# Feed-forward rows halved in row layout and turned by DMA instead of on TensorE

## The chip, the cores and the metric

The kernel runs on one NeuronCore of a Trainium2 chip. The metric is the device time of one execution in microseconds (us). The engines are TensorE (PE, with its weight loads shown as PEld), VectorE (DVE), ScalarE (ACT), GpSimd (POOL) and SyncE (SP), which here only issues DMAs.

## The reference

A gated block of a vision-language model, on 8 sequences of 224 rows of 2048 values, everything in float32:

```
x = x + tanh(g_xattn) * cross_attention(layernorm(x), ctx, ctx)     # 32 heads of 64, 8 shared key/value groups, 750 context rows
x = x + tanh(g_ffn) * ffn(layernorm(x))

ffn(h):  query = h @ Wq.T                       # 2048 -> 64
         top 8 of 512 router scores of query; softmax over those 8 slots gives w
         aux = (w @ aux_values) @ Wvd.T @ Wvu.T
         u = uncertainty(h)                     # variance of h, and gelu(h @ Wu1.T + bu1) @ Wu2.T, 2048 -> 512 -> 1
         return h + gate(u) * aux
```

Where bf16 is fed to TensorE, a float32 value is halved into a bf16 high part and a bf16 rest (value minus high part), and the product is summed from high*high, high*rest and rest*high.

## The kernel before

The attention takes the first 900 us or so and the change does not touch it. The feed-forward part then works on 14 tiles of 128 rows. Each engine has its own instruction stream written out by hand; the streams meet in semaphores, and an engine runs its stream strictly in order. After a lead-in for tiles 0 and 1 the streams have a loop `for t in range(1, TILES)`; loop t is called "loop t" below. It holds, for tile t, the query projection (`sum_query`), the wide projection (`sum_wide`), the router and the selection of 8 slots (`route`, `select`, `weigh`), for tile t - 1 the rest of the chain (`preact`, `gelu`, `dot`, `turn_w`, `sum_z`), and for tile t + 1 the preparation of the normed rows h. Loops 1 to 5 also carry the layer-norm statistics of later tiles on DVE (`late_stats`, two tiles a loop). Loops 8 to 13 and the part behind the loops carry the results of two tiles each (`FINISH`): eight quarters of 512 columns, each three matmuls on PE (`aux_part`), then one DVE instruction that adds it to the rows (`finish`); ACT prepares each of these tiles with one pass over its 2048 columns (`base`), and SP stores each finished tile.

The preparation of h is done in four quarters of 512 columns, j = 0 to 3. Before the change a quarter goes through these steps:

- `stage_h` (L1254, DVE): h = (x - mean) * rstd as float32, row layout, into `h_rows`, two buffers.
- `turn_h` (L953, PE): four float32 transposes of 128 by 128 into PSUM bank j % 2.
- `round_h` (L679, ACT): PSUM to bf16, the high part `h_hi`. It waits for the transposes and for `w1_quarter`, since tile t's `sum_wide(t, j)` must have read the quarter that is overwritten. There is one buffer per quarter.
- `split_h` (L1273, DVE): PSUM minus high part, to bf16 `h_lo`.
- `sum_query` (L980) and `sum_wide` (L966) on PE multiply the two parts.

`preact(t)` (L1362, DVE) empties the bank of `sum_wide(t, ...)` and `sum_wide(t + 1, 0)` waits for it; so in loop t the first quarter of `sum_wide` waits for `preact(t - 1)`, which is the first DVE instruction of the loop. `join_query` is L1366, `select` L1342 to L1354, `split_z` L1387, statistics L1240 and L1246, `finish` L1383 and `aux_part` L1044. On ACT, `gelu` is L766, `weigh` L770, `base` L745, `round_z` L778. All results' quarters but the last ones share PSUM bank 7, so that a quarter's matmuls wait for the DVE pass over the quarter before.

SP waits for each finished tile of `ORDER` and stores 1 MB (L490). The last two tiles are stored in quarters.

Of the kernel before, what the change touches and what calls it, by code (L numbers as in the profile page):

```python
# [5 lines left out]
ALU = mybir.AluOpType  # L6
# [62 lines left out]
def flamingo_block(nc, x_top, x_rest, k_t, v_rows, mask, g_x, av_t, wvd_t, w1_t, wq_t, wr, wr_rows_in, keys_t, log_rel, rel, b1, w2, wvu_t,  # L69
                   scalars, spill, out):  # L70
    with ExitStack() as ctx:
# [107 lines left out]
        h_rows = carve("ffn", [128, 2, 512])  # L179
        h_hi = carve("ffn", [128, 4, 4, 128], BF16)  # L180
        h_lo = carve("ffn", [128, 4, 4, 128], BF16)
        stage_at = used["ffn"] + 3 * HID
# [116 lines left out]
        h_hi_done = sem("h_hi_done")  # L299
        h_split = sem("h_split")  # L300
        w1_quarter = sem("w1_quarter")
        query_quarter = sem("query_quarter")
# [77 lines left out]
        def parts_before(u, n):  # L380
            return 4 * ORDER.index(u) + n

        TAIL_BANKS = {(TILES - 2, 0): 7, (TILES - 2, 1): 0, (TILES - 2, 2): 1, (TILES - 2, 3): 3,
                      (TILES - 1, 0): 4, (TILES - 1, 1): 5, (TILES - 1, 2): 2, (TILES - 1, 3): 7}

        def aux_ps(u, n):
            return psum[:, TAIL_BANKS.get((u, n), 7), :]

# [4 lines left out]
        def _(sp):  # L393
# [104 lines left out]
        def _(pool):  # L498
# [108 lines left out]
            pool.tensor_tensor(keys_lo[:, :], keys_raw, keys_hi[:, :], ALU.subtract).then_inc(keys_split, 1)  # L607

            for t in range(EARLY, TILES):
                root2(t, t + 1)  # L610

            pool.wait_ge(rstd2_done, TILES)
# [45 lines left out]
        def _(act):  # L658
# [16 lines left out]
            def round_h(t, j):  # L675
                act.wait_ge(h_turned, 4 * t + j + 1)
                if t >= 1:
                    act.wait_ge(w1_quarter, 4 * (t - 1) + j + 1)
                act.activation(h_hi[:, j], psum[:, j % 2, :].rearrange("p (k n) -> p k n", k=4), ACT.Copy).then_inc(h_hi_done, 1)  # L679

# [112 lines left out]
            for t in range(1, TILES):  # L793
                if t + 1 <= TILES:
                    round_h(t, 3)
                if t == 1:
# [5 lines left out]
                if t + 1 < TILES:  # L802
                    round_h(t + 1, 0)
                if t == LOG_STEP:
# [32 lines left out]
        def _(pe):  # L837
# [108 lines left out]
            def turn_h(t, j):  # L946
# [7 lines left out]
                mm.then_inc(h_turned, 1)  # L954

            def sum_wide(t, j, halves=range(2)):
                if 0 in halves:
                    pe.wait_ge(h_split, 4 * t + j + 1)
                    if t == 0:
                        pe.wait_ge(w1_split, 4 * j + 4)  # L960
                    if j == 0 and t >= 1:
                        pe.wait_ge(preact_done, t)
                for kk in range(2 * halves[0], 2 * halves[-1] + 2):
                    k = 4 * j + kk
                    for n, (h, w) in enumerate(((h_hi, high(w1_raw[:, k, :])), (h_hi, w1_lo[:, k, :]), (h_lo, high(w1_raw[:, k, :])))):
                        mm = pe.matmul(psum[:, 2, :], h[:, j, kk, :], w, start=(k == 0 and n == 0), stop=(k == KC - 1 and n == 2))  # L966
                if 1 in halves:
                    mm.then_inc(w1_quarter, 1)

            def sum_query(t, j):  # L970
                pe.wait_ge(h_split, 4 * t + j + 1)
                if t == 0 and j == 0:
# [47 lines left out]
            def aux_part(t, i):  # L1020
# [7 lines left out]
                if n == 0:  # L1028
                    pe.wait_ge(z_split, u + 1)
                bank = TAIL_BANKS.get((u, n), 7)  # L1030
                if bank == 7 and parts_before(u, n) >= 1:
                    last = parts_before(TILES - 2, 1) if (u, n) == (TILES - 1, 3) else parts_before(u, n)
                    pe.wait_ge(y_added, last)
                elif bank in (0, 1):
                    pe.wait_ge(h_split, 4 * TILES)
                elif bank == 3:
# [64 lines left out]
            for t in range(1, TILES):  # L1101
                last = t == TILES - 1
                sum_query(t, 0)
# [11 lines left out]
                sum_wide(t, 1, range(1, 2))  # L1115
                if not last:
                    turn_h(t + 1, 1)
                aux_part(t, 3)
# [4 lines left out]
                sum_wide(t, 2, range(1, 2))  # L1123
                if not last:
                    turn_h(t + 1, 2)
                aux_part(t, 5)
# [5 lines left out]
                sum_wide(t, 3, range(1, 2))  # L1132
                if not last:
                    turn_h(t + 1, 3)
                aux_part(t, 7)
# [10 lines left out]
        def _(dve):  # L1146
# [100 lines left out]

            def stage_h(t, j):
                rows = rows_of(t)
                if j == 0:  # L1250
                    dve.wait_ge(rstd2_done, t + 1)
                if t >= 1 or j >= 2:
                    dve.wait_ge(h_turned, 4 * t + j - 1)
                dve.tensor_scalar(h_rows[:, j % 2, :], rows[:, 512 * j:512 * j + 512], mv_all[:, t, 0:1], rstd_all[:, t:t + 1],  # L1254
                                  ALU.subtract, ALU.mult).then_inc(h_staged, 1)

            def next_stats(window, m):
# [153 lines left out]
            split_h(1, 2)  # L1411
            stage_h(2, 0)
            join_query(0)
            split_query(0)

            for t in range(1, TILES):
                preact(t - 1)
                finish(t - 1, 7)
                late_stats(t - 1, 7)
                split_h(t, 3)  # L1420
                if t + 1 < TILES:
                    stage_h(t + 1, 1)
                finish(t, 0)
# [4 lines left out]
                if t + 1 < TILES:  # L1428
                    split_h(t + 1, 0)
                    stage_h(t + 1, 2)  # L1430
                finish(t, 1)
# [8 lines left out]
                if t + 1 < TILES:  # L1440
                    split_h(t + 1, 1)
                    stage_h(t + 1, 3)
                finish(t, 3)
# [5 lines left out]
                if t + 1 < TILES:  # L1449
                    split_h(t + 1, 2)  # L1450
                if t + 2 < TILES:
                    stage_h(t + 2, 0)
                finish(t, 5)
# [91 lines left out]
```

## Time and profile before

| what | us |
|---|---|
| median of 3 runs (lowest, highest) | 1191.7 (1190.68, 1191.79) |
| the profiled execution's own time | 1189.83 |
| its span, first to last instruction | 1187.9 |
| busy in the span: PE, DVE, ACT, POOL | 1141.3, 946.4, 918.8, 888.4 |
| mean granted TensorE clock | 0.999 of full speed |

The span is what the profiler saw between the first and the last instruction; the execution's own time is 1.93 us longer. Busy time is the time in which an engine had an instruction under way; PE's is modelled from pipelined matmuls, so the distance between starts says more than the duration.

### The profile page before, as it was taken

The page shows a single profiled execution, that of the slowest core. Times are in us where ns is not written, and L with a number is a line of the kernel's source. Part 1 is how long each engine was busy: PE and PEld are TensorE (multiplying, and loading weights), DVE is VectorE, ACT ScalarE, POOL GpSimd, SP SyncE. Part 2 cuts the span into 40 slices and gives each one's busy share as a digit, 9 for nine tenths or more (in the row PEclk, how much of TensorE's full clock was granted, in tenths as well). Part 3 has the DMA queues.
Part 4 walks back from the last instruction along what each step waited for, and adds up shares of the span by engine and source line. Part 5 has one row for each costly group of instructions (what it writes and reads, how often), then busy time and mean ns, then how long its engine had stood idle before and what let it go on. Part 6 is the DMA issues. An engine that isn't in the chain of part 4 may idle for free.

```text
span 1187.9 us, 35060 instructions
## 1 busy us (share of the span) xinstructions
PE 1141.3 (96%) x14385; PEld 912.3 (77%) x14642; DVE 946.4 (80%) x2255; ACT 918.8 (77%) x1230; POOL 888.4 (75%) x797
## 2 busy tenths in 40 slices
PE   4999999999999999999999999999999999999997
PEld 3888888888888888888888888888877565555553
DVE  5988888887888888888888888888874888766765
ACT  5898998988988898898898889989862344555544
POOL 5999999999999999999999999999970001503222
PEclk9999999999999999999999999999999999999999
DMA  9421231142124213311421221131237100011223
GB/s 340 141 68 48 62 110 54 42 107 71 41 55 103 75 41 68 116 48 41 104 71 52 58 58 42 50 73 47 70 103 262 81 1 1 1 72 72 107 107 142
DMA packets 60735, 95.09 MB, mean 80 GB/s; under 512 B 35233, under 2 KB 44449, under 8 KB 56482
## 3 DMA queue, kind: packets, MB, share of 16 engines
q1 hardware_dynamic: 59858, 91.79, 25.1%
q8 instruction: 118, 1.93, 0.7%
q10 hardware_dynamic: 720, 1.05, 0.3%
q14 instruction: 39, 0.32, 0.1%
HBM read 71.75 MB, written 20.97 MB: 78 GB/s over the span
## 4 chain that ended last, share of the span: by engine, by line
PE 70%; POOL 16%; DVE 8%; issue 3%; ACT 2%; DMA 1%; DVEq 0%; SPq 0%; POOLq 0%
PE psum L913 13%; PE psum L890 12%; POOL arena L577 11%; PE psum L966 8%; PE psum L920 6%; PE psum L901 6%; PE psum L943 6%; PE psum L937 5%; PE psum L938 5%; PE psum L1044 2%; POOL arena L545 2%; PE psum L868 2%; PE psum L953 1%; PE psum L980 1%; POOL arena L594 1%
## 5 line engine op out<-in xcount | busy, mean ns | idle before, releaser
L577 POOL TENSOR_TENSOR arena<-arena 128x768 bf16<-128x768 f32 x448 | 652.6, 1472 | 43.4 <-ACT arena L699 41.5
L1283 DVE CUSTOM_DVE_ANT_0 arena<-psum,arena 128x750 f32<-128x750 f32 x448 | 420.5, 939 | 127.7 <-PE psum L901 122.0
L699 ACT ACTIVATE arena<-psum 128x768 f32<-128x768 f32 x448 | 362.6, 809 | 87.8 <-PE psum L920 87.7
L703 ACT ACTIVATE arena<-arena,neg_max 128x750 f32<-128x750 f32 x448 | 410.9, 917 | 4.2 <-DVE neg_max L1283 4.2
L913 PE MATMUL psum<-ident,arena 128*128 128x128 f32 x1792 | 268.4, 272 | 0.0
L937 PEld LDWEIGHTS psum<-arena 128*128 128x128 bf16 (+1 forms) x2688 | 194.7, 98 | 57.5
L890 PE MATMUL psum<-arena 128*128 128x512 bf16 x674 | 221.9, 383 | 14.2
L938 PE MATMUL psum<-arena 128*128 128x64 bf16 (+1 forms) x2688 | 222.0, 193 | 0.0
L937 PE MATMUL psum<-arena 128*128 128x65 bf16 (+1 forms) x2688 | 221.7, 194 | 0.0
L938 PEld LDWEIGHTS psum<-arena 128*128 128x128 bf16 (+1 forms) x2688 | 178.5, 98 | 53.2
L913 PEld LDWEIGHTS psum<-ident,arena 128*128 128x128 f32 x1792 | 206.3, 140 | 4.3
L920 PE MATMUL psum<-ident,arena 128*128 128x128 f32 x896 | 171.4, 273 | 0.9 <-ACT arena L699 0.7
L901 PE MATMUL psum<-arena 128*128 128x238 bf16 x896 | 167.2, 267 | 0.9 <-DVE neg_max L1283 0.9
L943 PE MATMUL psum<-arena 128*128 128x65 bf16 (+1 forms) x2688 | 159.9, 194 | 0.9 <-POOL arena L577 0.9
L966 PE MATMUL psum<-arena 128*128 128x512 bf16 x649 | 157.2, 384 | 3.7 <-DVE arena L1362 2.6
L966 PEld LDWEIGHTS psum<-arena 128*128 128x128 bf16 x672 | 63.5, 96 | 77.2 <-issue 3.0
L943 PEld LDWEIGHTS psum<-arena 128*128 128x128 bf16 (+1 forms) x2688 | 114.9, 98 | 1.5 <-POOL arena L577 1.4
L920 PEld LDWEIGHTS psum<-ident,arena 128*128 128x128 f32 x896 | 111.8, 141 | 1.8 <-ACT arena L699 1.6
L679 ACT ACTIVATE arena<-psum 128x512 bf16<-128x512 f32 x56 | 33.3, 597 | 101.0 <-PE psum L953 100.9
L1226 DVE SCALAR_TENSOR_TENSOR arena<-psum,r_den,arena 128x64 f32<-128x64 f32 x448 | 97.5, 278 | 2.3
L545 POOL TENSOR_TENSOR arena<-arena 128x750 bf16<-128x750 f32 x64 | 92.2, 1441 | 0.2
L890 PEld LDWEIGHTS psum<-arena 128*128 128x128 bf16 x896 | 88.0, 98 | 5.2
(160 smaller groups left out, 1267.6 us busy)
## 6 DMA issues: line engine op xcount, KB each, us to landing
arena<-in_k_t SPq DMA_DIRECT2D x128, 187.5 KB, 3.2
arena<-in_v_rows SPq DMA_DIRECT2D x64, 192.0 KB, 2.5
out<-arena SPq DMA_DIRECT2D x12, 1024.0 KB, 3.9
arena<-in_x_top SPq DMA_DIRECT2D x8, 1024.0 KB, 5.3
arena<-in_x_rest SPq DMA_DIRECT2D x8, 768.0 KB, 4.5
spill<-arena SPq DMA_DIRECT2D x96, 64.0 KB, 2.2
arena<-spill SPq DMA_DIRECT2D x6, 1024.0 KB, 7.2
arena<-in_w_t SPq DMA_DIRECT2D x4, 1024.0 KB, 19.9
```

The lines of the kernel that those rows point to most:

```text
L577: pool.tensor_tensor(p_lo[:, n % RING, :], p_sb[:, n % RING, :], high(p_sb[:, n % RING, :]), ALU.subtract).then_inc(p_split, 1)
L699: act.activation(p_sb[:, n % RING, :], flat_ps[:, turned_at(n):turned_at(n) + CW], ACT.Copy).then_inc(evac_a, 1)
L703: act.activation(s_sb[:, n % RING, 0:CTX], s_sb[:, n % RING, 0:CTX], ACT.Exp, bias=neg_max[:, n % 4, :], scale=-1.0).then_inc(exped, 1)
L890: pe.matmul(flat_ps[:, score_at(n) + cols.start:score_at(n) + cols.stop], q_t[:, pair % 2, half, turn, :], kk, start=(i == 0), stop=(i == 1))
L901: mm = pe.matmul(flat_ps[:, score_at(n) + cols.start:score_at(n) + cols.stop], q_t[:, g // 2 % 2, half, turn, :], kk, start=(i == 0), stop ...
L913: pe.transpose(flat_ps[:, at:at + 128], s_sb[:, n % RING, c * 128:(c + 1) * 128], ident[:, :])
L920: mm = pe.transpose(flat_ps[:, at:at + 128], s_sb[:, n % RING, c * 128:(c + 1) * 128], ident[:, :])
L937: pe.matmul(o, hi, v_hi[0:rows, u, c, :], start=(c == 0), stop=False, skip_group_check=True)
L938: pe.matmul(o[:, 0:D], hi, v_lo[0:rows, u, c, :], start=False, stop=False, skip_group_check=True)
L943: mm = pe.matmul(o, lo, v_hi[0:rows, u, c, :], start=False, stop=(c == NCH - 1), skip_group_check=True)
L966: mm = pe.matmul(psum[:, 2, :], h[:, j, kk, :], w, start=(k == 0 and n == 0), stop=(k == KC - 1 and n == 2))
L1283: dve.tensor_tensor_reduce(s_sb[:, n % RING, 0:CTX], flat_ps[:, score_at(n):score_at(n) + CTX], mask_sb[:, max(n % UNITS - REP + 1, 0), :] ...
```

## The change

The preparation of h for tiles 2 to 13 is done in row layout. ACT computes the high part straight from the rows (`Identity` with scale rstd and bias -mean * rstd), DVE computes the float32 value and then value minus high part, and both bf16 halves of a quarter lie side by side in one of two buffers `h_pairs` (128 x 1024 bf16, 256 KB). SP turns such a pair with one transposing DMA into `h_cat[:, j]`, which PE reads. PE's `turn_h` is gone from the loops. POOL computes the bias (`shift2`). The stores of finished tiles move behind quarter 0's DMA of a later tile, and the results' quarters rotate over PSUM banks 7, 0 and 1, of which 0 and 1 held the transposes.

```diff
+        h_cat = carve("ffn", [128, 4, 8, 128], BF16)
+        h_hi, h_lo = h_cat[:, :, 0:4, :], h_cat[:, :, 4:8, :]
+        h_pairs = (keys_raw.bitcast(BF16), h_rows[:, 1, :].bitcast(BF16))
...
+        def aux_bank(u, n):
+            part = parts_before(u, n)
+            last = part - (4 * TILES - 5)
+            return (3, 4, 5, 2, 7)[last] if last >= 0 else (7, 0, 1)[part % 3]
...                                                          # SP
-            for u in ORDER[:-2]:
-                sp.wait_ge(y_added, parts_before(u, 4))
-                sp.dma_start(out[u], rows_of(u)).then_inc(out_stored, 16)
+            for t in range(2, TILES):
+                for j in range(4):
+                    sp.wait_ge(h_split, 4 * t + j + 1)
+                    sp.wait_ge(w1_quarter, 4 * (t - 1) + j + 1)
+                    sp.dma_start_transpose(h_cat[:, j], h_pairs[j % 2]).then_inc(h_loaded[j], 16)
+                    if j == 0:
+                        for u in FINISH.get(t - 2, ()):
+                            sp.wait_ge(y_added, parts_before(u, 4))
+                            sp.dma_start(out[u], rows_of(u)).then_inc(out_stored, 16)
...                                                          # POOL
+            def shift2(t):
+                pool.wait_ge(rstd2_done, t + 1)
+                pool.tensor_scalar(shift_all[:, t:t + 1], mv_all[:, t, 0:1], rstd_all[:, t:t + 1], -1.0, ALU.mult, ALU.mult).then_inc(shift_done, 1)
...                                                          # ACT, round_h for t >= 2
+                if j >= 2:
+                    act.wait_ge(h_loaded[j - 2], 16 * (t - 1))
+                elif t >= 3:
+                    act.wait_ge(h_loaded[j + 2], 16 * (t - 2))
+                act.activation(h_pairs[j % 2][:, 0:512], rows_of(t)[:, 512 * j:512 * j + 512], ACT.Identity, bias=shift_all[:, t:t + 1],
+                               scale=rstd_all[:, t:t + 1]).then_inc(h_hi_done, 1)
...                                                          # ACT, loop t
                 if t + 1 < TILES:
-                    round_h(t + 1, 1)
+                    round_h(t + 1, 2)
                 round_z(t - 1)
                 if len(bases) > 1:
                     base(bases[1])
+                weigh(t)
                 if t + 1 < TILES:
-                    round_h(t + 1, 2)
-                weigh(t)
+                    round_h(t + 1, 3)
...                                                          # PE
+            def quarter_ready(t, j):
+                if t < 2:
+                    pe.wait_ge(h_split, 4 * t + j + 1)
+                else:
+                    pe.wait_ge(h_loaded[j], 16 * (t - 1))
...
-                if not last:
-                    turn_h(t + 1, 0)                         # likewise 1, 2, 3
...                                                          # PE, aux_part
+                if part == 4 * TILES - 1:
+                    pe.wait_ge(y_added, part - 6)
+                elif bank in (7, 0, 1) and part >= 3:
+                    pe.wait_ge(y_added, part - 2)
...                                                          # DVE, stage_h for t >= 2
+                if t >= 2:
+                    dve.wait_ge(h_staged, 4 * t + j + 1)
+                    dve.wait_ge(h_hi_done, 4 * t + j + 1)
+                    dve.tensor_tensor(h_pairs[j % 2][:, 512:1024], wide, h_pairs[j % 2][:, 0:512], ALU.subtract).then_inc(h_split, 1)
...                                                          # DVE, loop t: where split_h and stage_h stood
+                    stage_h(t + 1, 0)                        # behind preact, finish 7
...
+                    stage_h(t + 1, 1)                        # behind dot
...
+                    stage_h(t + 1, 2)                        # behind join_query, split_query, finish 2
...
+                    stage_h(t + 1, 3)                        # behind select, split_z, finish 4
```

## Rows read from the trace of the kernel before

**Rows 1.** Busy time by loop: window us, its length, busy us and instructions by engine
```profile
909.57:935.45 25.88, 25.19 (x185) 17.40 (x187) 17.85 (x36) 9.92 (x18) 0.75 (x2) 1.00 0.57 225
970.00:987.28 17.28, 16.70 (x114) 10.18 (x114) 15.01 (x32) 7.75 (x14) 1.62 (x4) 1.00 0.00 0
1004.56:1022.43 17.87, 15.88 (x96) 9.14 (x96) 14.44 (x27) 8.48 (x14) 7.11 (x12) 1.00 0.00 1
1022.43:1039.26 16.83, 16.70 (x112) 10.16 (x113) 10.12 (x22) 11.67 (x15) 11.37 (x19) 1.00 0.00 1
1039.26:1061.44 22.18, 21.64 (x132) 12.16 (x134) 14.90 (x29) 11.88 (x16) 0.00 (x0) 1.00 0.12 48
1084.29:1107.14 22.85, 22.31 (x135) 12.45 (x137) 15.55 (x29) 11.83 (x15) 6.15 (x18) 1.00 0.23 93
```

**Rows 2.** Timeline, PE's weight loads in loop 4: start us, duration us, group
```profile
973.26 0.58 PEld L953 LDWEIGHTS psum<-ident,arena 128*128 128x128 f32 x4
973.82 0.47 PEld L1054 LDWEIGHTS psum<-ident,arena 128*128 128x128 f32 x4
```

**Rows 3.** Timeline, DVE in loop 4; in brackets idle time before it
```profile
970.00 0.67 DVE L1362 TENSOR_TENSOR arena<-psum,arena 128x512 f32<-128x512 f32 x1
...
978.74 0.69 DVE L1273 TENSOR_TENSOR arena<-psum,arena 128x512 bf16<-128x512 f32 x1 [0.67 <-ACT arena L679]
...
980.71 0.64 DVE L1342 MAX8 top<-psum 128x8 f32<-128x512 f32 x1
...
984.24 0.29 DVE L1387 TENSOR_TENSOR arena<-psum,arena 128x128 bf16<-128x128 f32 x1
984.44 0.69 DVE L1240 BATCH_NORM_STATS2 bn<-arena 128x6 f32<-128x512 f32 x1
985.04 0.67 DVE L1273 TENSOR_TENSOR arena<-psum,arena 128x512 bf16<-128x512 f32 x1
985.63 0.54 DVE L1254 TENSOR_SCALAR arena<-arena,mv_all,rstd_all 128x512 f32<-128x512 f32 x1
986.09 1.28 DVE L1240 BATCH_NORM_STATS2 bn<-arena 128x6 f32<-128x512 f32 x2
987.28 0.67 DVE L1362 TENSOR_TENSOR arena<-psum,arena 128x512 f32<-128x512 f32 x1
```

**Rows 4.** Timeline, PE: first quarter of the wide projection in loops 4, 1 and 10
```profile
971.05 2.60 PE L966 MATMUL psum<-arena 128*128 128x512 bf16 x11 [0.52 <-DVE arena L1362]
...
918.68 2.60 PE L966 MATMUL psum<-arena 128*128 128x512 bf16 x11
...
1087.20 2.83 PE L966 MATMUL psum<-arena 128*128 128x512 bf16 x12
```

**Rows 5.** Timeline, ACT: weigh in loop 1, the second base pass in loop 10
```profile
932.52 0.72 ACT L770 ACTIVATE arena<-arena,neg_top 128x512 f32<-128x512 f32 x1 [0.36 <-DVE neg_top L1354]
933.15 0.19 ACT L770 ACTIVATION_READ_ACCUMULATOR arena<-arena,neg_top 128x1 f32 x1
...
1098.84 2.09 ACT L745 ACTIVATE arena<-arena,base_bias,base_scale 128x2048 f32<-128x2048 f32 x1
```

**Rows 6.** DMA issues, whole run: KB each, median us from issue to landing
```profile
out<-arena SPq DMA_DIRECT2D x12, 1024.0 KB, 3.9
spill<-arena SPq DMA_DIRECT2D x96, 64.0 KB, 2.2
arena<-in_wvd_t SPq DMA_DIRECT2D x8, 128.0 KB, 7.6
out<-arena SPq DMA_DIRECT2D x4, 256.0 KB, 3.1
ln_mv<-mv_rest SPq DMA_DIRECT2D x28, 0.8 KB, 2.2
```

**Rows 7.** Timeline, DVE in loop 6: one staging instruction
```profile
1009.92 3.87 DVE L1254 TENSOR_SCALAR arena<-arena,mv_all,rstd_all 128x512 f32<-128x512 f32 x1
```

**Rows 8.** Waits, 1061 to 1153 us (loops 9 to 12): us in total, times, longest
```profile
PEld psum L1044 <- DVE arena L1383: 3.9, 7, 0.6
```

More of the change, by code:

```diff
@@ L300, in flamingo_block @@
         h_split = sem("h_split")
+        h_loaded = [sem(f"h_loaded{j}") for j in range(4)]
+        shift_done = sem("shift_done")
         w1_quarter = sem("w1_quarter")
@@ L487, in _ @@
                 sp.dma_start(x2b[:, i, :], spill[128 * i:128 * i + 128]).then_inc(x2_loaded[i], 16)
-            for u in ORDER[:-2]:
-                sp.wait_ge(y_added, parts_before(u, 4))
-                sp.dma_start(out[u], rows_of(u)).then_inc(out_stored, 16)
+            for t in range(2, TILES):
[7 more added lines that the diff above has]
+                            sp.dma_start(out[u], rows_of(u)).then_inc(out_stored, 16)
+            for t in (TILES - 2, TILES - 1):
+                for u in FINISH.get(t, ()):
+                    sp.wait_ge(y_added, parts_before(u, 4))
+                    sp.dma_start(out[u], rows_of(u)).then_inc(out_stored, 16)
             for u in ORDER[-2:]:
@@ L607, in _ @@
             pool.tensor_tensor(keys_lo[:, :], keys_raw, keys_hi[:, :], ALU.subtract).then_inc(keys_split, 1)
+            def shift2(t):
+                pool.wait_ge(rstd2_done, t + 1)
+                pool.tensor_scalar(shift_all[:, t:t + 1], mv_all[:, t, 0:1], rstd_all[:, t:t + 1], -1.0, ALU.mult, ALU.mult).then_inc(shift_done, 1)
+            for t in range(2, EARLY):
+                shift2(t)
             for t in range(EARLY, TILES):
                 root2(t, t + 1)
+                shift2(t)
             pool.wait_ge(rstd2_done, TILES)
@@ L675, in round_h @@
             def round_h(t, j):
[L676 to L679, printed above, removed]
+                if t < 2:
+                    act.wait_ge(h_turned, 4 * t + j + 1)
+                    if t >= 1:
+                        act.wait_ge(w1_quarter, 4 * (t - 1) + j + 1)
+                    act.activation(h_hi[:, j], psum[:, j % 2, :].rearrange("p (k n) -> p k n", k=4), ACT.Copy).then_inc(h_hi_done, 1)
+                    return
+                if j == 0:
+                    act.wait_ge(shift_done, t - 1)
+                if j >= 2:
[3 more added lines that the diff above has]
+                else:
+                    act.wait_ge(keys_split, 2)
+                    act.wait_ge(h_turned, 8)
+                act.activation(h_pairs[j % 2][:, 0:512], rows_of(t)[:, 512 * j:512 * j + 512], ACT.Identity, bias=shift_all[:, t:t + 1],
+                               scale=rstd_all[:, t:t + 1]).then_inc(h_hi_done, 1)
             def round_q(bank, pair, half, turns, count):
@@ L793, in _ @@
             for t in range(1, TILES):
[L794 to L795 removed]
+                if t == 1:
+                    round_h(1, 3)
+                if t + 1 < TILES:
+                    round_h(t + 1, 0)
                 if t == 1:
@@ L1029, in aux_part @@
                     pe.wait_ge(z_split, u + 1)
[L1030 to L1035, printed above, removed]
+                bank, part = aux_bank(u, n), parts_before(u, n)
+                if bank in (0, 1) and part < 3:
+                    pe.wait_ge(h_split, 8)
+                if part == 4 * TILES - 1:
+                    pe.wait_ge(y_added, part - 6)
+                elif bank in (7, 0, 1) and part >= 3:
+                    pe.wait_ge(y_added, part - 2)
                 elif bank == 3:
@@ L1251, in stage_h @@
                     dve.wait_ge(rstd2_done, t + 1)
-                if t >= 1 or j >= 2:
-                    dve.wait_ge(h_turned, 4 * t + j - 1)
-                dve.tensor_scalar(h_rows[:, j % 2, :], rows[:, 512 * j:512 * j + 512], mv_all[:, t, 0:1], rstd_all[:, t:t + 1],
+                if t < 2:
+                    if t >= 1 or j >= 2:
+                        dve.wait_ge(h_turned, 4 * t + j - 1)
+                elif (t, j) == (2, 0):
+                    dve.wait_ge(h_turned, 7)
+                else:
+                    dve.wait_ge(h_split, 4 * t + j)
+                wide = h_rows[:, j % 2 if t < 2 else 0, :]
+                dve.tensor_scalar(wide, rows[:, 512 * j:512 * j + 512], mv_all[:, t, 0:1], rstd_all[:, t:t + 1],
                                   ALU.subtract, ALU.mult).then_inc(h_staged, 1)
+                if t >= 2:
+                    dve.wait_ge(h_staged, 4 * t + j + 1)
+                    dve.wait_ge(h_hi_done, 4 * t + j + 1)
+                    dve.tensor_tensor(h_pairs[j % 2][:, 512:1024], wide, h_pairs[j % 2][:, 0:512], ALU.subtract).then_inc(h_split, 1)
             def next_stats(window, m):
```

34 lines of the change are left out of this document (9 added, 25 removed).

## The prediction, on record before the result

> **What bounds the kernel now.** I cut the part behind 909 us at each `preact`, the first DVE instruction of a loop, and read the busy times of the pieces [rows 1]. The reader is to see three kinds of loops. Loops 2 to 5 (four of 17.28 us, one is shown) have PE busy for 16.70 and DVE for 15.01 us: two engines close together. Loops 6 and 7 have no statistics; loop 7 is PE's alone (16.70 of 16.83). In loops 9 to 12 (four of 22.7 to 22.9 us) PE is busy for 22.3 and DVE for 15.6 us. In the timeline of loop 4, DVE begins `preact` at 970.00 without having waited and PE then shows 0.52 us idle before the first quarter of the wide projection, released by it [rows 3, 4]. So loops 2 to 5 are set by a ring: preact, wide projection, h of the next tile, selection, preact. From loop 6 on PE is late everywhere.
>
> **What goes from PE.** The weight loads of four transposes start at 973.26, those of the next group at 973.82 [rows 2]: a quarter's transposes take 0.56 us of PE, not the sum of four durations. They stood in loops 1 to 12, four to a loop: 2.2 us a loop. Nothing takes their place on PE. The rotation of the results over three banks removes the waits of PE for DVE's pass over the quarter before: 3.9 us in four loops [rows 8]. I count half of it as lost again to the loads' own start, 0.5 us a loop. So the PE bound is 16.83 - 2.2 = 14.6 us in loops 6 and 7, and 22.85 - 2.75 = 20.1 in loops 9 to 12.
>
> **What it adds.** Each quarter now goes ACT, DVE, SP, DMA, PE. ACT's pass reads SBUF instead of PSUM and POOL's twelve one-column instructions run where POOL is 2 to 11 us busy in 17 to 23 [rows 1]: no cost. DVE does the same instructions as before, but the rest must follow its own float32 value, so that the value takes 0.58 us (0.54 and a semaphore) where the next instruction used to start after 0.46 [rows 3]: 0.5 us a loop, inside the ring below. The new item is the time L from the end of DVE's rest to the landing of the turned pair. No row shows a transposing DMA. From below: the smallest transfer and one in pieces of 256 B land in 2.2 us, 256 KB in rows of 2 KB in 3.1 [rows 6]. From above, by the slowest of these rows: 7.6. The pair is 256 KB too, but I assume 1024 pieces of 256 B and a crossbar in the way. I take 4.5, nearest to the 256 KB store, with 1.4 us for the pieces; this is the weakest number of the forecast, and everything below is written in L.
>
> The Trainium skill, page "DMA: Bandwidth & Descriptors", section "Latency and other measured facts", gives 261 GB/s for a transposing DMA. That makes 1.0 us of 256 KB and, with a 2.2 us floor, an estimate of L = 3.2 and a time of about 1166 us. No row here shows it.
>
> **The ring of loops 2 to 5.** There is one `h_cat`, so quarter 0's DMA waits for the wide projection to have read quarter 0, and only two pair buffers, so ACT's high part of quarter 2 waits for that DMA to land. From `preact` (0): quarter 0 of the wide projection ends at 971.05 + 2.60 - 970.00 = 3.65 [rows 3, 4]; SP 0.1; L; ACT 0.6 and two semaphores. DVE starts quarter 2's rest at 4.5 + L, if it has come there: its own way (preact, three statistics, quarters 0 and 1, dot, the joined query, the value of quarter 2), with the steps of loop 4, takes 7.95. What stands behind it in DVE's order: rest 0.60, statistics with merge 0.90, select 3.53 (980.71 to 984.24), z 0.20, statistics 0.60, value 0.58, rest of quarter 3 0.60, two statistics 1.19 [rows 3]. Before that last rest ACT has to finish `weigh`, which now stands ahead of quarter 3's high part: 0.94 us behind the selection, then 0.6 [rows 5], against 1.38 of DVE: 0.2 us of waiting. Sum 8.4. The loop is 12.9 + L, never under 16.35. At L = 4.5: 17.4, against 17.28. So the 2.2 us that PE gives up are worth nothing here: + 0.5 us for the four. Quarter 3's DMA starts at about 16.2 and lands at 20.8, which is 3.4 into the next loop; PE wants it at 4.1. It is free up to L of about 5.
>
> **The other loops.** Loop 1: PE works on the value projection until 917 us, and quarter 0 ends at 921.3 [rows 4]; + 0.75 + L + 8.4 gives 934.9 at L = 4.5, against 935.45: - 0.5. Loops 6 and 7: without three statistics and the merge behind quarter 2, but with 0.76 of waiting for ACT, 6.3 us follow it; in loop 7 the wide quarter ends 3.9 behind preact; the loop is 11.0 + L = 15.5, above PE's 14.6: - 1.3 in loop 7 and - 2.4 in loop 6. In loop 6 a staging instruction takes 3.87 us [rows 7] while POOL has its long pass; in the new order DVE would wait for quarter 2 there anyway.
>
> Loops 8 to 12: the wide quarter ends at 1087.20 + 2.83 - 1084.29 - 0.55 = 5.2 [rows 4]; quarter 2's rest starts at 6.0 + L; then rest, a finish, select (together 4.9), `weigh` and the high part on ACT (1.6), rest, two finishes (2.0): 14.5 + L = 19.0 at 4.5. ACT's second `base` pass of 2.09 us [rows 5] with z and the table load ahead of `weigh` raises this to about 19.8, whatever L up to 5.3. PE's 20.1 is later, by little: - 2.75 in each of loops 9 to 12 and - 2.2 in loop 8, - 13.2. The stores: two of 1 MB now go to SP's queue right behind quarter 0's DMA (tiles 10 to 13); at 3.9 us for one [rows 6] and some 2.6 more for the second they are through at 11.8 in the loop, where quarter 1's DMA is issued at 10, and ACT needs that buffer at 16.5. Hidden; without the slack it would be 1 to 2 us in each of four loops. Loop 13 has no preparation: - 0.6 by the banks, and - 0.4 in the end.
>
> **Sum.** -0.5 + 0.5 - 2.4 - 1.3 - 13.2 - 1.0 = -17.9 us. The profiled execution took 1189.83 (span 1187.9), so 1171.9 for one like it; it lay 1.9 under the median of the runs. 1191.7 - 17.9 = 1173.8, forecast 1174. In L the change is 7L - 49.4 up to 5.5, and 12L - 77.3 above, where loops 8 to 12 join the ring.
>
> **Rivals.**
> - *A slow turn (slower).* The change costs time as soon as L passes 77.3 / 12 = 6.4 us. Place: ACT's wait for `h_loaded` before quarter 2, and DVE behind it. For it: a landing row of 7.6 us, and small pieces. Against it: 256 B pieces land in 2.2. At 7.6 it costs 13.9: 1206. The extreme in rows is a pair turned as eight blocks of 128 columns, one after the other, each at the 2.2 us floor: L = 17.6, + 134, 1326.
>   The Trainium skill has that mechanism as a price: "VectorE: DVE Perf Modes", section "The three transpose paths", gives 1309 ns for one 128 by 128 block turned by a DMA. Eight in turn are an estimate of L = 10.5, and 12 x 10.5 - 77.3 = + 49 us, 1240. No row shows it; I give it 1 in 10, inside this rival.
> - *Turns don't overlap.* If the four DMAs of a tile can't be in flight together a loop is at least 4L. At 4.5 that is 18.0: loops 2 to 5 + 2.9, loop 6 + 0.1, loop 7 + 1.2, the rest as above: -10.5, 1181. For it: one queue. Against it: two 1 MB transfers overlap their fixed parts.
> - *A quick turn.* Under L = 3.45 DVE's own way bounds loops 2 to 5 at 16.35 and PE loops 6 and 7 at 14.6: loops 2 to 5 - 3.7, loop 1 - 1.5, loops 6 and 7 - 5.5, the rest - 14.2: 1167 at most, down to 1163 if all of the bank waits go.
> - *The cover in loops 8 to 12 is thinner than I think* (19.8 against 20.1): 1 us more on ACT or DVE gives back 0.7 in five loops, 1178. It is inside the forecast's own range.
>
> **Chances.** Forecast, L from 3.5 to 5.5, 1167 to 1181: 0.43. Quick turn, 1163 to 1167: 0.10. No overlap, or L from 5.5 to 6.3, 1181 to 1189: 0.13. L about 6.4, no change: 0.05. Slow turn: 0.29, of which 0.12 lies under 1206. A measurement of this kernel can tell 0.2% (2.4 us) from no change; faster than that 0.66, within it 0.05, slower 0.29. The range is 1163 to 1206: it leaves out 0.17 above and 0.03 below.
>
> **What would show it.** The landing time of the transposing DMA in the DMA issues is L itself. Loops 2 to 5 should be 12.9 + L apart from preact to preact, with DVE idle before the rest of quarter 2, released by ACT, and ACT idle before that quarter's high part, released by a DMA; PE should be idle before the wide quarter 0. Loops 9 to 12 should be 20.1 us with PE busy for nearly all of it and no bank waits on `aux_part`. PE should have 192 transposes of the rows fewer. It is wrong if DVE's rest from two SBUF operands isn't about 0.6 us, if loops 9 to 12 show PE idle before the query projection (quarter 2 or 3 late), or if L is above 6.4.

## The result and the profile after

| | before | after |
|---|---|---|
| median of 4 runs (lowest, highest), us | 1191.21 (1190.68, 1191.79) | 1175.30 (1174.31, 1176.21) |
| profiled execution's own time, span, us | 1189.83, 1187.9 | 1174.31, 1172.5 |

The ratio is 0.9865, 95% interval 0.9849 to 0.9881: 15.9 us faster by the medians. The forecast was 1174, a gain of 17.9, but several of its terms were wrong and cancelled. A turn is one transposing DMA of 256 KB below, and L is the time from its issue to its landing. Cut as before at each `preact` (L1410 in the new numbering):

| loop | 1 | 2 | 3 to 5, each | 6 | 7 | 8 | 9 to 12, sum | 13 | end |
|---|---|---|---|---|---|---|---|---|---|
| before, us | 25.88 | 17.28 | 17.28 | 17.87 | 16.83 | 22.18 | 91.25 | 21.42 | 13.8 |
| after, us | 28.62 | 17.99 | 16.35 | 17.16 | 15.37 | 19.13 | 81.61 | 20.40 | 13.6 |
| difference | +2.7 | +0.7 | -0.9 | -0.7 | -1.5 | -3.1 | -9.6 | -1.0 | -0.2 |
| forecast | -0.5 | +0.1 | +0.1 | -2.4 | -1.3 | -2.2 | -11.0 | -0.6 | -0.4 |

These are lines of the profile page after, parts 1 and 2. PE's busy time falls by only 3.3 us on the page, but this is no measure of the change: the trace before lacks matmul records. Up to 909.5 us, where the kernels do the same, it has 12738 matmuls and 877.6 us of busy PE, and the trace after has 12963 and 892.7. From `preact` of loop 1 to `preact` behind loop 13 PE is busy for 256.3 us before and 237.9 after. The DMA packets grow by 50,688, which is 1056 for each of 48 turns, all of them under 512 B; the forecast had assumed 1024 pieces of 256 B.

```profile
PE 1138.0 (97%) x14450; PEld 892.6 (76%) x14450; DVE 948.4 (81%) x2255; ACT 927.1 (79%) x1230; POOL 899.4 (77%) x809
...
DMA packets 111423, 107.66 MB, mean 92 GB/s; under 512 B 85921, under 2 KB 95137, under 8 KB 107170
```

The busy times of loops 1, 2, 3, 6, 7, 8 and 10, with the columns of [rows 1]. Loop 3 has DVE at 15.21 and PE at 15.23 of 16.36, and neither is full; loops 8 and 10 have PE at 100%. Loop 2 alone has a granted clock of 0.91.

```profile
909.61:938.23 28.62, 24.25 (x179) 16.04 (x177) 18.65 (x38) 12.29 (x19) 1.01 (x3) 1.00 0.67 224
938.23:956.22 17.99, 16.87 (x96) 8.80 (x96) 15.29 (x32) 7.68 (x14) 3.19 (x6) 0.91 0.31 59
956.22:972.58 16.36, 15.23 (x96) 8.41 (x96) 15.21 (x32) 8.62 (x14) 3.19 (x6) 1.00 0.35 66
1005.28:1022.44 17.16, 15.37 (x98) 8.64 (x98) 14.30 (x28) 9.91 (x16) 7.59 (x11) 1.00 0.33 61
1022.44:1037.81 15.37, 14.54 (x87) 7.91 (x88) 10.12 (x23) 11.38 (x15) 11.94 (x19) 1.00 0.43 70
1037.81:1056.94 19.13, 19.13 (x107) 9.72 (x105) 15.05 (x29) 13.16 (x16) 0.48 (x2) 1.00 0.30 56
1077.35:1097.75 20.40, 20.40 (x121) 10.71 (x120) 15.75 (x30) 12.59 (x15) 6.64 (x18) 1.00 0.60 156
```

The DMA issues answer to [rows 6]. The first line is L: 3.1 us from issue to landing (median of 48), as for the 256 KB store in rows of 2 KB before. The 1 MB stores, which now run beside turns, take 5.9 us instead of 3.9.

```profile
arena<-arena SPq DMA_TRANSPOSE x48, 3.1
...
out<-arena SPq DMA_DIRECT2D x12, 1024.0 KB, 5.9
```

The Trainium skill, page "DMA: Bandwidth & Descriptors", section "Latency and other measured facts", gave with a 2.2 us floor an estimate of 3.2 us for this transfer; the trace agrees, with 3.1. The price that the Trainium skill gives on the page "VectorE: DVE Perf Modes", section "The three transpose paths" (1309 ns for one 128 by 128 block), times eight blocks, gave 10.5 us; the trace does not bear that multiplication out.

**Loops 3 to 5** answer to [rows 3, 4]. These are lines of DVE in loop 3. The rest of quarter 2 starts at 963.99 with no idle time before it, and in the whole loop DVE waits only for 0.38 and 0.41 us.

```profile
956.22 0.68 DVE L1410 TENSOR_TENSOR arena<-psum,arena 128x512 f32<-128x512 f32 x1
...
962.47 0.28 DVE L1418 TENSOR_TENSOR arena<-arena 64x128 bf16<-64x128 f32 x1 [0.38 <-ACT arena L799]
...
963.40 0.53 DVE L1298 TENSOR_SCALAR arena<-arena,mv_all,rstd_all 128x512 f32<-128x512 f32 x1
963.99 0.69 DVE L1303 TENSOR_TENSOR arena<-arena 128x512 bf16<-128x512 f32 x1
...
970.78 0.69 DVE L1303 TENSOR_TENSOR arena<-arena 128x512 bf16<-128x512 f32 x1 [0.41 <-ACT arena L715]
971.38 1.28 DVE L1277 BATCH_NORM_STATS2 bn<-arena 128x6 f32<-128x512 f32 x2
972.58 0.68 DVE L1410 TENSOR_TENSOR arena<-psum,arena 128x512 f32<-128x512 f32 x1
```

ACT still waits 0.64 us for quarter 0's turn. Its high part ends at 963.89 and DVE's value of the quarter at 963.93, so the ring and DVE's own way reach the rest of quarter 2 within 0.1 us of each other. PE, which before the change was close to a bound, now waits 1.12 us for `preact`.

```profile
963.08 0.81 ACT L715 ACTIVATE arena<-arena,shift_all,rstd_all 128x512 bf16<-128x512 f32 x1 [0.64 <-DMA arena<-arena]
...
957.04 2.83 PE L1011 MATMUL psum<-arena 128*128 128x512 bf16 x12 [1.12 <-DVE arena L1410]
```

**Loops 1 and 2.** The lines are of SP, ACT, DVE and PE. SP has issued three `spill` loads of 1 MB (L494, the rows of tiles 11 to 13) at 917.46, before the first turn at 921.51; the last of the three lands at about 927.6 and the turn at 928.7, 7.2 us after its issue. ACT waits 3.96 us for that turn, DVE 3.39 us behind ACT, and PE stands still for 4.24 us before loop 2's wide quarter 0.

```profile
917.46 1.28 SPq L494 DMA_DIRECT2D arena<-spill  x3
921.51 5.93 SPq L499 DMA_TRANSPOSE arena<-arena  x2
...
928.72 0.81 ACT L715 ACTIVATE arena<-arena,shift_all,rstd_all 128x512 bf16<-128x512 f32 x1 [3.96 <-DMA arena<-arena]
...
929.64 0.69 DVE L1303 TENSOR_TENSOR arena<-arena 128x512 bf16<-128x512 f32 x1 [3.39 <-ACT arena L715]
...
939.05 4.47 PE L1011 MATMUL psum<-arena 128*128 128x512 bf16 x12 [4.24 <-DVE arena L1410]
```

These twelve matmuls take 4.47 us where loop 3's take 2.83. The busy times in pieces (columns of [rows 1]) show a granted clock of 0.62 and 0.71 of full speed right after that idle time, a mean between the 1.2 and the 2.4 GHz level, and full speed again later:

```profile
936.00:939.00 3.00, 0.00 (x0) 0.00 (x0) 2.60 (x6) 2.38 (x4) 0.00 (x0) 1.00 0.24 46
939.00:942.00 3.00, 2.95 (x9) 1.15 (x10) 2.93 (x6) 1.38 (x2) 1.94 (x3) 0.62 0.23 42
942.00:944.00 2.00, 2.00 (x13) 1.10 (x11) 1.88 (x5) 0.01 (x1) 0.25 (x1) 0.71 0.00 0
944.00:956.00 12.00, 11.92 (x80) 6.55 (x77) 9.49 (x20) 5.91 (x11) 1.00 (x3) 1.00 0.35 66
```

**Loop 6** answers to [rows 7]. Quarter 2's value takes 3.63 us on DVE beside POOL's one long pass (L648). ACT's high part had been ready since about 1012.9, so the rest starts some 2.6 us late.

```profile
1011.66 3.65 POOL L648 TENSOR_TENSOR arena<-arena 128x2048 bf16<-128x2048 f32 x1
...
1011.97 3.63 DVE L1298 TENSOR_SCALAR arena<-arena,mv_all,rstd_all 128x512 f32<-128x512 f32 x1
1015.63 0.69 DVE L1303 TENSOR_TENSOR arena<-arena 128x512 bf16<-128x512 f32 x1
```

**Loop 7.** ACT's pass for quarter 1 of the next tile waits for the landing of quarter 3 of the tile before, which shares its pair buffer, and DVE waits 1.75 us behind it. That turn, issued at 1022.28, took 3.9 us instead of 3.1; why is not known. DVE then waits 1.90 us more for quarter 2, whose high part stands behind ACT's `base` pass of 2.08 us.

```profile
1026.21 0.81 ACT L715 ACTIVATE arena<-arena,shift_all,rstd_all 128x512 bf16<-128x512 f32 x1 [2.11 <-DMA arena<-arena]
...
1027.13 0.69 DVE L1303 TENSOR_TENSOR arena<-arena 128x512 bf16<-128x512 f32 x1 [1.75 <-ACT arena L715]
```

**Loops 9 to 12** answer to [rows 8]: in the waits of 1056.94 to 1138.55 no line has PE waiting for DVE's pass over a results' quarter. What is left between them is DVE waiting for PE:

```profile
DVE arena L1431 <- PE psum L1090: 5.7, 12, 0.7
```

### The profile page after: what moved, and what is told of

Its sections match the earlier page's. It is cut to its first block, busy times and chain, and to the rows that moved or that the text cites. A ratio compares the mean times of both kernels' runs of the same rounds, so it can differ in the third digit from the quotient of the medians.

```text
span 1172.5 us, 35006 instructions
## 1 busy us (share of the span) xinstructions
PE 1138.0 (97%) x14450; PEld 892.6 (76%) x14450; DVE 948.4 (81%) x2255; ACT 927.1 (79%) x1230; POOL 899.4 (77%) x809
## 4 chain that ended last, share of the span: by engine, by line
PE 66%; POOL 19%; DVE 7%; DMA 3%; issue 2%; ACT 2%; SPq 1%; DVEq 0%; POOLq 0%; ACTq 0%
POOL arena L594 14%; PE psum L929 12%; PE psum L952 12%; PE psum L1011 7%; PE psum L959 6%; PE psum L940 6%; PE psum L982 5%; PE psum L976 5%; PE psum L977 5%; PE psum L1090 3%; POOL arena L562 2%; PE psum L907 2%; DVE bn L1277 1%; POOL arena L611 1%; POOL arena L602 1%
## 5 line engine op out<-in xcount | busy, mean ns | idle before, releaser
L929 PE MATMUL psum<-arena 128*128 128x512 bf16 x896 | 272.4, 385 | 0.0
L1011 PE MATMUL psum<-arena 128*128 128x512 bf16 x672 | 162.0, 387 | 10.5 <-DVE arena L1410 10.5
L1217 DVE TENSOR_TENSOR arena<-psum,arena 64x384 bf16<-64x384 f32 (+2 forms) x130 | 79.9, 614 | 6.2 <-ACT arena L720 2.2
```

The costliest lines, as they stand in the source:

```text
L929: pe.matmul(flat_ps[:, score_at(n) + cols.start:score_at(n) + cols.stop], q_t[:, pair % 2, half, turn, :], kk, start=(i == 0), stop=(i == 1))
```

## Experiments

Diffs are against the kernel after unless they say otherwise. Kernels timed together share the runs of the kernel before, whose medians were 1190.31 us (e1 to e4), 1190.6 (e5, e6, e7, e9) and 1190.26 (e8, e10). Times below are medians.

**The bank rotation by itself.** My theory priced it at 0.5 us a loop and PE's transposes at 2.2.

```diff
-            return (3, 4, 5, 2, 7)[last] if last >= 0 else (7, 0, 1)[part % 3]
+            return (3, 4, 5, 2, 7)[last] if last >= 0 else {-2: 0, -1: 1}.get(last, 7)
...                                              # and the wait for the quarter before on bank 7
```

> The changed kernel, but the results' quarters stay in PSUM bank 7 as before (banks 0, 1 only near the end as before). Theory of the prediction: the rotation gives 0.5 us in each of loops 8 to 12 and 0.6 in loop 13, so this is 3 us slower than the changed kernel, about 1178, with PE idle on the pass over the quarter before. Rival: without the transposes between them the results' matmuls follow each other more closely and one bank costs 1 us a loop or more: 1181 and above. Other rival: DVE keeps up, under 1 us.

Measured: 1184.1 us, ratio 0.9948 (0.9933 to 0.9963). Loops 9 to 12 are 21.88 or 21.89 each, against 20.40 with three banks and 22.85 before. Removing the transposes was worth 0.97 us a loop by itself, and the rotation 1.5 on top of it; what the rotation would give without that removal wasn't run. The waits of loops 9 to 12 (us in total, times, longest) show where the difference went: with fewer matmuls between two results' quarters PE comes to the bank earlier. Its weight loads wait for 8.6 us in four loops, where the line of [rows 8] had 3.9, and its matmuls for 4.6, where they had 1.4. The two overlap and don't add up: PE is idle for 4.6 us of these four loops.

```profile
PEld psum L1090 <- DVE arena L1431: 8.6, 8, 1.2
...
PE psum L1090 <- DVE arena L1431: 4.6, 8, 0.7
```

**The loads ahead of the first turn.** Two ways to take the three 1 MB loads from between the first turns: one behind each of tiles 2 to 4, then the same in quarters of 256 KB, one behind each turn.

```diff
-            for i in range(3, B_TILES):
-                sp.dma_start(x2b[:, i, :], spill[128 * i:128 * i + 128]).then_inc(x2_loaded[i], 16)
...                                              # e1: behind the four turns of tile t
+                if t in (2, 3, 4):
+                    i = t + 1
+                    sp.dma_start(x2b[:, i, :], spill[128 * i:128 * i + 128]).then_inc(x2_loaded[i], 16)
...                                              # e9: behind each turn j of tile t; DVE waits for 64 in place of 16
+                    if t in (2, 3, 4):
+                        i, cols = t + 1, slice(512 * j, 512 * j + 512)
+                        sp.dma_start(x2b[:, i, cols], spill[128 * i:128 * i + 128, cols]).then_inc(x2_loaded[i], 16)
```

> The three 1 MB loads of tiles 11 to 13 are issued one each behind quarter 3's turn of tiles 2, 3 and 4, no longer all ahead of the first turn. Theory (queue): the first turn landed 7.2 us after issue because it lay behind these loads; it will land in about 3.1, ACT's wait of 3.96 us in loop 1 goes, loop 1 falls from 28.6 to about 24.6, PE no longer idles 4.2 us and its clock stays full, so loop 2 falls from 18.0 to 16.4. Total 5 to 6 us less than the changed kernel: about 1170. Rival (first turn is slow by itself, or the ring of loop 1 needs its time): the first landing stays near 7 us and the total within 1 us of 1175. Second rival: each load now delays a turn of its own by 2 to 4 us, total 1175 to 1180.

Measured: 1172.11 us, ratio 0.9847 (0.9832 to 0.9861). Loops 1 and 2 are 25.55 and 16.36 (4.7 us gained in this trace), but loops 3 and 4 became 17.78 and 18.0 (3.1 lost). In loop 3 a load was issued at 951.25, 3.5 us before the next turn. It took 7.1 us, the turn behind it landed after 4.5, and ACT waited 2.06 us for it; DVE waited behind it, PE then idled 2.54 us before the wide quarter of loop 4, and its matmuls took 4.46 us at a granted clock of 0.91 over the loop. The lines are of SP, ACT and PE of this kernel, and its loop 4:

```profile
951.25 0.57 SPq L504 DMA_DIRECT2D arena<-spill  x1
954.78 4.78 SPq L497 DMA_TRANSPOSE arena<-arena  x2
...
959.32 0.81 ACT L716 ACTIVATE arena<-arena,shift_all,rstd_all 128x512 bf16<-128x512 f32 x1 [2.06 <-DMA arena<-arena]
...
969.65 4.46 PE L1012 MATMUL psum<-arena 128*128 128x512 bf16 x12 [2.54 <-DVE arena L1411]
...
968.83:986.83 18.00, 16.86 (x96) 8.84 (x96) 15.30 (x33) 7.70 (x14) 3.20 (x6) 0.91 0.48 117
```

So the disturbance moved with a load. It isn't every load: the other two took 5.4 and 5.2 us, and the turns behind them landed after 3.1. In both kernels a delayed turn landed 0.9 to 1.1 us after the 1 MB ahead of it had landed (928.7 after 927.6 in loop 1 of the kernel after, 959.3 after 958.35 here). Why one load took 7.1 us isn't known.

> The three 1 MB loads of tiles 11 to 13 cut into quarters of 256 KB, one behind each turn of tiles 2, 3 and 4. With whole loads behind quarter 3's turn two of the three made the next turn land late, PE then idled 2.5 us and ran at the lower clock level for a stretch. Theory (queue position and amount ahead of a turn): a quarter load is through before the next turn is issued 3 us later; loop 1 stays at 25.5, loops 2 to 5 all at 16.36 with full clock; total 1169 to 1170. Rival (a transposing DMA is slow next to any transfer): turns land later in all of loops 1 to 4 and the total is 1172 or more.

Measured: 1169.47 us, ratio 0.9819 (0.9805 to 0.9834). Loops 1 to 5 are 25.73, 16.37, 16.36, 16.36 and 16.36: both disturbances are gone, and so is the lower clock. Of e1's whole loads one had delayed a turn, not two as expected above. A quarter load lands after 3.2 to 4.1 us, and no turn of loops 1 to 5 takes more than 3.5. PE still waits 0.88 us before loop 2's wide quarter and its twelve matmuls take 2.83 us again:

```profile
936.18 2.83 PE L1012 MATMUL psum<-arena 128*128 128x512 bf16 x12 [0.88 <-DVE arena L1411]
```

**A longer L.** Each quarter is turned by two DMAs of 128 KB, all else equal.

```diff
-                    sp.dma_start_transpose(h_cat[:, j], h_pairs[j % 2]).then_inc(h_loaded[j], 16)
+                    for part in range(2):
+                        sp.dma_start_transpose(h_cat[:, j, 4 * part:4 * part + 4],
+                                               h_pairs[j % 2][:, 512 * part:512 * part + 512]).then_inc(h_loaded[j], 16)
...                                              # waits on h_loaded count 32 a tile
```

> Each quarter is turned by two DMAs of 128 KB (high parts, then rests) instead of one of 256 KB; SP issues them one after the other, so the second is issued 1.23 us later. Ring theory: the landing that everything waits for comes about 1.2 us later if the cost is SP's issue, and loops 2 to 5 and 7 grow by that (DVE waits for ACT before quarter 2's rest), loops 8 to 12 by about 0.7 since there is next to no slack; 9 to 11 us in all, 1185. Rival (DVE's own way bounds loops 2 to 5, PE loops 8 to 12): the later landing is covered and the time moves under 2 us. If the issue time goes with the amount (0.6 us each), no change either, and the landing says so.

Measured: 1184.17 us, ratio 0.9942 (0.9926 to 0.9959). One half lands in 2.5 us (median), and SP issues the second 1.24 us behind the first. From the first issue to ACT's pass for quarter 2 that makes 3.8 us in loops 2, 3 and 5. In loop 4 the second half took 4.1 us, and it is 984.09 - 978.74 = 5.35, where the kernel after has 963.08 - 959.95 = 3.13. Why single halves take longer isn't known. The lines are of ACT and DVE in loop 4:

```profile
984.09 0.81 ACT L717 ACTIVATE arena<-arena,shift_all,rstd_all 128x512 bf16<-128x512 f32 x1 [2.86 <-DMA arena<-arena]
...
985.01 0.69 DVE L1305 TENSOR_TENSOR arena<-arena 128x512 bf16<-128x512 f32 x1 [2.29 <-ACT arena L717]
```

Loops 2 to 5 are 19.31, 17.27, 18.57 and 18.67. Only loop 4 tests the ring of the prediction cleanly: 12.9 + L gives 18.25 at 5.35, against 18.57. Its pieces are 3.72 us from `preact` to the issue, 5.35, then 0.92 to DVE's rest and 8.58 to the next `preact`, so the ring is 13.2 + L, with the path that was forecast. Loops 2 and 5 also hold a stretch of lower clock (0.85 and 0.91 over the loop, after 3.93 and 2.86 us without a matmul). In loop 3 another landing counts: ACT waits 2.75 us for quarter 3 of the tile before, ahead of its pass for quarter 1. Loops 8 to 12 stay at 19.5 and 20.1 to 20.8, so their cover is thicker than I had worked out.

**DVE's own way.** Two of the four late statistics of each tile left out.

```diff
-                bank_stats(u, c)
+                if c in (0, 3):
+                    bank_stats(u, c)
                 if c == 3:
                     merge2(u)
```

> Leaves out two of the four statistics instructions of each late tile (columns 512 to 1535), four a loop in loops 1 to 5, 0.60 us each. Rival that DVE's work alone bounds loops 3 to 5 (16.36): they fall by 1.8 to PE's 14.6. Ring theory: the two ahead of quarter 2 are hidden behind the turn, the two behind it count: 4.7 + 3.1 + 7.4 = 15.2 to 15.3, with DVE idle about 1.2 us before quarter 2's rest. Total 4 to 6 us less, the loop time decides.

Measured: 1168.7 us, ratio 0.9821 (0.9807 to 0.9836). Loops 2 to 5 are 15.15, 15.75, 15.49 and 15.16. The four instructions left out of a loop are 2.4 us of DVE, but the loops fall by at most 1.2, which is the two that stand behind quarter 2. The lines are of ACT and DVE in loop 5, and of PE in loop 2:

```profile
990.36 0.81 ACT L715 ACTIVATE arena<-arena,shift_all,rstd_all 128x512 bf16<-128x512 f32 x1 [1.17 <-DMA arena<-arena]
...
991.27 0.69 DVE L1303 TENSOR_TENSOR arena<-arena 128x512 bf16<-128x512 f32 x1 [1.19 <-ACT arena L715]
...
937.94 2.83 PE L1011 MATMUL psum<-arena 128*128 128x512 bf16 x12 [3.28 <-DVE arena L1410]
```

DVE now waits 1.19 us for the turned quarter: this is the ring, 3.73 + 3.13 + 0.91 + 7.39 = 15.16 (from `preact` to the issue at 987.23, L, ACT's pass, and DVE's part behind it). In loop 3 of the kernel after the same sum is 3.73 + 3.13 + 0.91 + 8.59 = 16.36. So in loops 3 to 5 of the kernel after DVE's own way and the ring end together, and by these sums shortening one of them alone gains nothing. In loops 3 and 4 other waits add 0.3 to 0.6. Loop 1 stays at 28.11, which DVE's statistics therefore did not set.

**POOL's long pass.** The split of the value matrix `wvu` goes ahead of POOL's loops, in the kernel after (e5) and in the kernel before (e8).

```diff
+            pool.wait_ge(wvu_loaded, 16)
+            pool.tensor_tensor(wvu_lo, wvu, high(wvu), ALU.subtract).then_inc(wvu_split, 1)
             for t in range(EARLY, TILES):
                 root2(t, t + 1)
...                                              # and the same two lines gone from their old place
```

> POOL's one long pass (the rest of the last weight, 128x2048, 3.65 us) is done before the first loop instead of in loop 6, where DVE's value of quarter 2 took 3.63 us beside it. Theory: that instruction goes back to 0.5 us, DVE waits for the landed quarter only, loop 6 falls from 17.2 by about 2.6 to 14.6 or a little over, total 1172.7. Rival (my prediction's: DVE would have waited for quarter 2 there anyway): loop 6 stays within 0.5 us of 17.2. Other rival: the pass hurts the lead-in by as much.

Measured: 1174.84 us, ratio 0.9867 (0.9852 to 0.9882), no change that can be told from the kernel after. The step is visible in the trace all the same: quarter 2's value takes 0.54 us again and loop 6 falls from 17.16 to 14.89. But loop 7 rises from 15.37 to 16.31 and loop 1 from 28.62 to 29.47, and the whole run gains 0.5.

```profile
1012.61 0.54 DVE L1298 TENSOR_SCALAR arena<-arena,mv_all,rstd_all 128x512 f32<-128x512 f32 x1
1013.69 0.69 DVE L1303 TENSOR_TENSOR arena<-arena 128x512 bf16<-128x512 f32 x1 [0.54 <-ACT arena L715]
```

> The kernel before the change, with POOL's long pass (128x2048) done ahead of the first loop. Before, PE waited 1.40 us in loop 6 for the joined query behind DVE's 3.87 us staging instruction. Theory: loop 6 falls from 17.87 to about 16.5, total 1.3 us less than before, 1189.3: the fault was there before the change and is worth less there. Rival: the gain is as in the changed kernel's loop 6, 2.3 us or more. Other rival: nothing, since the lead-in pays it back.

Measured: 1188.6 us, ratio 0.9984 (0.9975 to 0.9993), 10 runs. Loop 6 falls from 17.87 to 16.21, loop 7 stays at 16.82, loop 1 grows by 0.17. So the staging instruction beside POOL's pass cost the kernel before 1.7 us in loop 6, and the kernel after 2.3 in that loop. Over loops 6 to 8 the two gains are 1.7 and 1.5: the change didn't make it dearer.

**The order on ACT.** Quarter 3's high part ahead of `weigh`, as it stood before the change.

```diff
-                weigh(t)
                 if t + 1 < TILES:
                     round_h(t + 1, 3)
+                weigh(t)
```

> ACT computes the high part of quarter 3 ahead of weigh instead of behind it. Theory: DVE's wait of 0.4 us (loops 3 to 5) and 1.0 us (loops 6, 7) before quarter 3's rest goes; loops 2 to 5 fall from 16.36 to 15.95, loops 6 and 7 by up to 1, loops 8 to 12 stay at 20.4 since PE is busy for all of them; total 2.5 to 3.5 us less than the changed kernel, 1172. Rival: DVE's wait moves to another place (the landed quarter 1) and nothing is won.

Measured: 1172.64 us, ratio 0.985 (0.9834 to 0.9867). Loops 3 to 5 fall to 15.99, by the 0.37 to 0.41 us that DVE waited there. Loops 6, 7 and 8 are 16.19, 15.95 and 19.75: their sum of 51.9 is that of the kernel after (51.7), and PE is idle for 2.6 us of it in both. The waits moved from one loop to another.

**All of these together.**

> Quarter loads, the early pass on POOL and quarter 3's high part ahead of weigh together. If the three causes are separate places of the timeline their gains add up: 5.5 + 2.6 + 3 = about 11 us under the changed kernel, 1164 to 1165, with loops 2 to 5 near 15.9, loops 6 and 7 near 14.6, loops 9 to 13 at 20.4. Rival: loops 6 and 7 stay on the landing of quarter 2 (15.3) and the sum is 9.

Measured: 1166.61 us (1166.08 to 1167.08), ratio 0.9798 (0.9783 to 0.9812); it holds e9, e5 and e6. Loops 1 to 5 are 25.61 and four of about 16.0, loops 6 to 8 are 14.89, 15.65 and 19.74. With the next one this is the best version: 8.7 us under the kernel after by the medians, and 0.7% less time by the two ratios.

> Quarter loads and the early pass on POOL, with quarter 3's high part ahead of weigh in loops 1 to 6 only. With the order changed in all loops, loops 7 and 8 had grown by 0.6 each, where ACT has two long passes: there weigh then comes late. Theory: loops 2 to 5 16.0, loop 6 14.9, loop 7 15.4 to 15.7, loop 8 19.1, loops 9 to 13 20.4: 0.6 to 1 us less than the version with all three in every loop, about 1165.8. Rival: loop 8 grows for another reason and the total stays at 1166.6.

Here the order was swapped back only up to loop 6. Measured: 1167.03 us, ratio 0.9801 (0.9788 to 0.9815), the same as e7. Loops 6 to 8 are 14.89, 16.38 and 18.99. The last loop's gain is the middle one's loss: the three loops sum to 50.3 in both, and to 50.2 in e5. These are loops 6 to 8 of e7 and of e10:

```profile
999.28:1014.17 14.89, 14.12 (x79) 7.51 (x79) 11.39 (x28) 9.33 (x15) 4.53 (x12) 1.00 0.38 70
1014.17:1029.82 15.65, 15.24 (x100) 8.34 (x98) 10.30 (x21) 12.36 (x15) 10.32 (x16) 1.00 0.37 69
1029.82:1049.56 19.74, 19.74 (x118) 10.31 (x116) 15.28 (x28) 13.16 (x16) 2.08 (x3) 1.00 0.29 54
```

```profile
999.93:1014.82 14.89, 14.02 (x78) 7.51 (x79) 11.40 (x28) 9.33 (x15) 4.52 (x12) 1.00 0.38 70
1014.82:1031.20 16.38, 15.86 (x112) 9.10 (x112) 10.22 (x21) 12.60 (x16) 11.05 (x16) 1.00 0.36 66
1031.20:1050.19 18.99, 18.87 (x102) 9.55 (x102) 15.01 (x30) 13.05 (x16) 0.59 (x3) 1.00 0.33 56
```

## Why the prediction was right, and where only its sum was

- *L, the landing of a turn.* Taken as 4.5 us, measured 3.1. At 3.1 the forecast's own rival "a quick turn" holds and gives 24.9 us less, 1167 at most. The loops of the profiled executions gained 15.4. The 9.5 us between them are loop 1 (4.2: -1.5 against +2.7), loop 2 (1.6: -0.9 against +0.7), loops 6 and 7 (3.3: -5.5 against -2.2) and the rest (0.3). So the likeliest case was not the one that came about: its time was hit by luck, because L was taken too long, and a queue, a clock and a POOL pass were missed.
- *Loops 2 to 5, "never under 16.35".* Loops 3 to 5 are 16.35 or 16.36. The floor, DVE's own way summed from [rows 3], was right to 0.01, by two errors that cancel: 7.77 us to the rest of quarter 2 instead of 7.95, and 8.59 behind it instead of 8.4. The ring was taken 0.3 too short (13.2 + L, measured in e3, with ACT's pass at 0.81 instead of 0.6 among it), so that at L = 3.1 it ends together with DVE's way, as e4 showed, and not 0.35 below it.
- *Loop 1.* The step that failed: I let quarter 0's turn start behind PE's wide quarter and counted L, without asking what was already in the DMA queue. SP's three loads of 1 MB stand ahead of it in SP's order. The turn landed 7.2 us after its issue. e9 gives 4.5 us back in loops 1 and 2 (28.62 + 17.99 against 25.73 + 16.37), 5.8 on the median and 5.5 by the two ratios.
- *Loop 2.* Nothing in the forecast let an idle PE cost more than the idle time. After 4.2 us without a matmul its wide quarter took 1.6 us longer at a lower granted clock. In e9, with 0.9 us of idle time there, it did not. The length of the idle time alone doesn't decide it: in e1 the clock fell after 2.54 us, and in e4 it stayed full after 3.28.
- *Loop 6, "DVE would wait for quarter 2 there anyway".* Wrong: at L = 3.1 the high part was ready, and the 3.63 us instruction stood in the ring. It cost 2.3 us in the loop (e5) and 1.5 over loops 6 to 8, where PE's idle time falls from 2.6 to 1.1 us. The median keeps 0.5 of it, which can't be told from nothing. Loop 1 lost 0.9 in that trace, where the first turn was issued 0.7 us later. Why is not settled; in e7 and e10, without loads ahead of that turn, the early pass costs loop 1 nothing.
- *Loop 7.* Forecast -1.3 and measured -1.5, but by another chain. I had quarter 3's landing awaited by PE at 4.1 us into the next loop. ACT awaits it first, for quarter 1 of the next tile, and the loop stays 0.8 us above PE's 14.6.
- *ACT's pass* takes 0.81 us from SBUF with tensor scale and bias, not the 0.6 of the pass from PSUM. It lies in the ring, and in loops 3 to 5 it is part of the 0.4 us that e6 took away.
- *Loops 8 to 12.* -12.7 against -13.2, as a sum of two wrong terms. The transposes were counted at 2.2 us a loop and are worth 0.97 by themselves; the rotation was counted at 0.5 and is worth 1.5. The mistake was to take the bank waits of [rows 8] as fixed: in e2 they grew when work between two results' quarters was taken away. With both, PE is busy for 20.40 of 20.40, not 20.1, so that the two together gave 2.4 us a loop, hardly more than the transposes' 2.2. The 0.5 was priced too high from the start: [rows 8] are waits of the weight loads, and PE's own were 1.4 us in four loops. Part of PE's idle time in [rows 1] is missing records, with 135 matmuls beside 137 weight loads in loop 10.
- *The stores* behind quarter 0's turn are hidden, as forecast, although one now takes 5.9 us and the turn behind the two takes 5.6 to 5.8 in each of loops 9 to 12 (issued at 1087.61 in loop 10, for example).

## What to carry to other kernels

When work is taken from a bounding engine, its short waits on another engine grow into the room; price them again at the new pace, and lift them in the same change. A transfer that becomes part of a ring has to be followed through its queue, at every place where something large may be in flight ahead of it: cutting those loads in quarters was worth more here (5.8 us) than any reordering on the engines. A loop that gets shorter ahead of a stretch that one engine fills is worth only the idle time that this engine loses over both (e5: 2.3 us in loop 6, 1.5 over three loops; e6: 1.0 and nothing). And where two paths end together, as in loops 3 to 5, a gain on one of them alone doesn't show.

## What was not expected of the hardware

- A transposing DMA of 256 KB, SBUF to SBUF in bf16, lands 3.1 us after its issue, and its issue holds SP for 1.23 us. Half of it takes 2.5 us, and two halves in a row 3.8 us in three loops and 5.35 in one, so that cutting it loses (1184.17 against 1175.30 us).
- Behind three 1 MB loads, the last issued 3.2 us earlier, the same turn took 7.2 us, behind one slow load 4.5, and behind two 1 MB stores 5.6 to 5.8. Each time it landed 0.9 to 1.2 us after the last of them had. Two other 1 MB loads, issued 3.5 and 5.2 us ahead, delayed nothing (3.1).
- After 4.24 and 2.54 us without a matmul PE's next twelve 512-column matmuls took 4.47 and 4.46 us; after 1.12 and 0.88 us they took 2.83, but so they did in e4 after 3.28.
- A float32 `tensor_scalar` of 128 x 512 on DVE, 0.54 us alone, took 3.63 us beside a POOL `tensor_tensor` of 128 x 2048. It started 0.3 us after POOL's and ended 0.3 us after it.
